# A four-layer graph network in 32 pipelined turns: a small product by rows, new instruction lists, and set-up steps moved into the first turn

## What is computed

```python
# a and d (4 heads of 64)
attn = softmax(where(adj, (q @ k.T) * 64 ** -0.5, -max))
out = (attn @ v) @ Wo + bo
# g (4 heads)
Wh = h @ W[h].T + bW[h]
scores = (Wh @ attn[h]) @ Wh.T
hp = relu(tanh(where(adj, scores, 0)) @ Wh)
ha, hf = concat(hp) @ A_w.T, h @ fc_w.T
coeff = sigmoid(hf @ g1_w.T + ha @ g2_w.T + gbias)
out = hf * coeff + ha * (1 - coeff)
# b (8 heads of 32)
m = x @ map_w.T + map_b
adj_h = (cos(m, m) > 0.1) * softmax(mask(q @ k.T / sqrt(32))) * keep
out = relu(adj_h @ (x @ gcn_map_w.T) @ gcn_W.T / (sum(adj_h) + 1))
```

## Time and profile before

| | us |
|---|---|
| median of 3 runs | 2783.31 |
| the profiled execution | 2784.76 |
| its span, first to last instruction | 2782.9 |
| PE busy in the span | 2662.1 (96%) |
| DVE, ACT, POOL busy | 1972.8, 1398.4, 908.0 |

### The profile page before, as it was taken

How to read it: one execution, slowest core, us unless ns; L and a number is a source line. 1 busy time by engine, 2 the same in 40 slices (tenths; PEclk the granted TensorE clock), 3 DMA queues, 4 the chain that set the end, 5 groups by cost and what they waited for, 6 DMA issues and landing times.

```text
span 2782.9 us, 62595 instructions
## 1 busy us (share of the span) xinstructions
PE 2662.1 (96%) x21777; PEld 2332.1 (84%) x21777; DVE 1972.8 (71%) x6629; ACT 1398.4 (50%) x3861; POOL 908.0 (33%) x979
## 2 busy tenths in 40 slices
PE   8799999999999999999999999999999999999985
PEld 7788888888888888888898888888888889888873
DVE  2367777778777767777777777777877777777764
ACT  1355445555454545544555545554554554554542
POOL 1223233432323333323343233333332434332331
PEclk8899999999999999999999999999999999999996
DMA  4000000000000000000000000000000000000000
GB/s 128 6 3 11 1 11 10 9 9 9 0 9 9 9 9 9 9 0 9 9 9 9 9 0 9 9 9 9 9 4 6 9 9 9 9 9 0 10 5 8
DMA packets 44481, 29.77 MB, mean 11 GB/s; under 512 B 21264, under 2 KB 44048, under 8 KB 44432
## 3 DMA queue, kind: packets, MB, share of 16 engines
q1 hardware_dynamic: 44432, 29.13, 3.6%
HBM read 20.73 MB, written 8.39 MB: 10 GB/s over the span
## 4 chain that ended last, share of the span: by engine, by line
PE 69%; DVE 21%; issue 5%; ACT 3%; DVEq 1%; POOL 0%; DMA 0%; SPq 0%; ACTq 0%; POOLq 0%
PE bank L247 13%; PE bank L249 12%; PE bank L248 12%; PE bank L246 9%; PE bank L1139 4%; PE bank L324 4%; PE bank L236 4%; PE bank L313 3%; PE bank L1121 3%; DVE b L420 2%; DVE x L170 2%; PE bank L1149 2%; DVE arena L420 2%; DVE b L463 2%; DVE l_st L158 2%
## 5 line engine op out<-in xcount | busy, mean ns | idle before, releaser
L1533 POOL TENSOR_TENSOR arena_r<-a,arena_r 128x512 fp32r<-128x512 f32 x128 | 166.0, 1297 | 585.0 <-ACT arena_r L1229 585.0
L1279 ACT ACTIVATE b<-b,s_sh 128x256 f32<-128x256 f32 x512 | 253.7, 499 | 116.0 <-DVE s_sh L420 116.0
L178 POOL TENSOR_SCALAR l_ve<-l_mv 128x2 f32<-128x2 f32 x128 | 29.0, 227 | 864.2 <-DVE l_mv L163 861.8
L247 PE MATMUL bank<-arena_r 128*128 128x256 f32 x1024 | 301.4, 294 | 1.8 <-POOL arena_r L1538 1.8
L248 PE MATMUL bank<-arena_r 128*128 128x256 f32 x1024 | 289.8, 283 | 0.0
L249 PE MATMUL bank<-arena_r 128*128 128x256 f32 x1024 | 289.5, 283 | 0.0
L1538 POOL TENSOR_TENSOR arena_r<-a,arena_r 128x512 fp32r<-128x512 f32 x128 | 165.5, 1293 | 174.6 <-ACT arena_r L1223 172.1
L247 PEld LDWEIGHTS bank<-arena_r 128*128 128x128 f32 x1024 | 195.6, 191 | 22.5 <-issue 20.6
L420 DVE CUSTOM_DVE_ANT_0 b<-bank,s_add 128x256 f32<-128x256 f32 x512 | 183.4, 419 | 39.9 <-PE bank L1121 39.0
L1439 DVE SCALAR_TENSOR_TENSOR b<-bank,b 128x256 f32<-128x256 f32 x512 | 185.1, 416 | 20.3 <-PE bank L1130 20.0
L249 PEld LDWEIGHTS bank<-arena_r 128*128 128x128 f32 x1024 | 196.1, 191 | 0.0
(11 more groups left out here) (273 smaller groups left out, 9099.4 us busy)
## 6 DMA issues: line engine op xcount, KB each, us to landing
x_in<-in_x SPq DMA_DIRECT2D x32, 256.0 KB, 2.8
out<-x SPq DMA_DIRECT2D x32, 256.0 KB, 2.1
adj_a<-in_adj SPq DMA_DIRECT2D x32, 64.0 KB, 2.5
adj_b<-in_adj SPq DMA_DIRECT2D x32, 64.0 KB, 2.4
a<-in_L_gnn_W SPq DMA_DIRECT2D x4, 256.0 KB, 3.3
b<-in_L_gnn_A_w SPq DMA_DIRECT2D x1, 1024.0 KB, 7.1
arena<-in_L_gnn_attn SPq DMA_DIRECT2D x4, 256.0 KB, 7.2
g_b_wh<-in_L_gnn_bW SPq DMA_DIRECT2D x1, 512.0 KB, 9.2
```

The lines of the kernel that those rows point to most:

```text
L247: pe.matmul(out, w[0], x[0], start=first, stop=False)
L1279: last = act.activation(S.e[:, n, it, :], S.e[:, n, it, :], ACT.Exp, bias=S.sh[:, it, h:h + 1], scale=-1.0, accum_out=S.sums[:, it, h:h + 1])
L1533: pool.tensor_tensor(G.wh[h % 2][1], G.whf[:, h % 2, :, :], G.wh[h % 2][0].bitcast(F32), ALU.subtract).then_inc(G.wh_sb.sem, 1)
```

## The change

- `g_c` takes the 8 columns of both halves of `w_c` as the stationary operand and x's halves as the moving one: 4 matmuls give 8 rows of 256. ACT copies the rows, and a new PE stage `g_c_t` has two plain fp32 matmuls that turn them and add the two halves by a selection matrix `C.sel` (8 x 4). DVE's stage is now called `g_c_t`.
- All four lists of `ORDER` are new. On PE the turn begins at `b_transpose_6`; ACT and DVE lists begin elsewhere in the turn than they did, so their lags differ by one.
- `FILL` and `DRAIN` are written-out lists for the turns before and after the hardware loop, which runs t = 4 to 30.
- Of the 34 set-up steps, 21 stay (`EARLY_COPIES`); 13 become stages `w_map` to `w_col_w` of `FILL` and use the four banks of `b` and `d`. PE has them before `a_k` of graph 0, DVE has `w_sem` and `w_col_w` after `a_stats`. What waited for all copies and `wr_loaded` at the end of set-up now waits at `g_x_t` of graph 0 (PE, DVE, ACT) or `a_bias` (POOL). SP loads the `bW` columns with `loads_a`, then the four weights of layer `a`, then `load_a(0)`.

The diff, cut to its core (DVE's and ACT's `late` follow PE's):

```diff
--- before.py
+++ after.py
@@ -49,51 +49,263 @@
 ORDER = {
     "PE": [
-        ("g_ha_3_1", 1), ("g_ha_3_0", 1), ("d_k", 2), ("g_ha_t", 1), ("a_x_t", 0), ("g_gate_x", 1), ("d_q", 2),
-        ("g_gate", 1), ("d_scores_0", 2), ("d_v", 2), ("a_k", 0), ("d_scores_1", 2), ("a_q", 0), ("a_v", 0),
-        ("a_scores_0", 0), ("d_probs_0", 2), ("d_probs_1", 2), ("d_probs_2", 2), ("d_probs_3", 2), ("a_scores_1", 0),
-        ("d_values_0", 2), ("b_x_t", 1), ("a_probs_0", 0), ("a_probs_1", 0), ("d_values_1", 2), ("a_probs_2", 0),
-        ("a_probs_3", 0), ("a_values_0", 0), ("a_values_1", 0), ("d_out", 2), ("a_out", 0), ("b_m", 1), ("b_sem", 1),
-        ("g_adj_t", 0), ("b_q", 1), ("g_x_t", 0), ("b_k", 1), ("g_z_0", 0), ("b_unit_t", 1), ("g_c", 0),
-        ("b_scores_0", 1), ("g_wh_0", 0), ("g_z_1", 0), ("g_s_0", 0), ("b_cos_0", 1), ("g_wh_1", 0), ("g_s_1", 0),
-        ("b_transpose_0", 1), ("b_transpose_1", 1), ("b_transpose_2", 1), ("b_transpose_3", 1), ("g_wh_2", 0),
-        ("b_values_0", 1), ("g_z_2", 0), ("b_scores_1", 1), ("g_p_0", 0), ("g_s_2", 0), ("g_z_3", 0), ("b_cos_1", 1),
-        ("g_p_1", 0), ("b_transpose_4", 1), ("g_wh_3", 0), ("b_transpose_5", 1), ("b_transpose_6", 1), ("g_s_3", 0),
-        ("b_transpose_7", 1), ("g_p_2", 0), ("b_values_1", 1), ("g_hf", 0), ("b_out", 1), ("g_ha_0_1", 0),
-        ("g_ha_0_0", 0), ("g_ha_1_1", 0), ("g_ha_1_0", 0), ("g_p_3", 0), ("g_ha_2_0", 0), ("g_ha_2_1", 0),
-        ("d_x_t", 1),
+        ("b_transpose_6", 2), ("b_transpose_7", 2), ("g_p_3", 1), ("b_values_1", 2), ("g_ha_2_1", 1), ("g_ha_3_1", 1),
+        ("b_out", 2), ("g_ha_2_0", 1), ("g_ha_3_0", 1), ("g_hf", 1), ("g_ha_t", 1), ("g_gate_x", 1), ("a_x_t", 0),
+        ("d_x_t", 2), ("g_gate", 1), ("d_q", 2), ("d_k", 2), ("d_v", 2), ("d_scores_0", 2), ("d_scores_1", 2),
+        ("a_v", 0), ("a_k", 0), ("a_q", 0), ("d_probs_0", 2), ("d_probs_1", 2), ("a_scores_0", 0), ("d_probs_2", 2),
+        ("a_scores_1", 0), ("d_probs_3", 2), ("d_values_0", 2), ("d_values_1", 2), ("a_probs_0", 0), ("a_probs_1", 0),
+        ("b_x_t", 1), ("a_probs_2", 0), ("a_probs_3", 0), ("a_values_0", 0), ("a_values_1", 0), ("d_out", 2),
+        ("a_out", 0), ("b_m", 1), ("b_q", 1), ("b_sem", 1), ("g_x_t", 0), ("g_adj_t", 0), ("b_k", 1), ("g_c", 0),
+        ("g_wh_0", 0), ("g_c_t", 0), ("g_z_0", 0), ("b_unit_t", 1), ("g_wh_1", 0), ("b_scores_0", 1), ("g_z_1", 0),
+        ("g_s_0", 0), ("g_wh_2", 0), ("b_cos_0", 1), ("g_z_2", 0), ("b_transpose_0", 1), ("g_s_1", 0), ("g_p_0", 0),
+        ("b_transpose_1", 1), ("b_transpose_2", 1), ("g_z_3", 0), ("b_transpose_3", 1), ("g_wh_3", 0),
+        ("b_values_0", 1), ("g_s_2", 0), ("b_scores_1", 1), ("g_s_3", 0), ("g_p_1", 0), ("g_ha_0_0", 0),
+        ("g_ha_0_1", 0), ("b_cos_1", 1), ("g_p_2", 0), ("g_ha_1_0", 0), ("b_transpose_4", 1), ("b_transpose_5", 1),
+        ("g_ha_1_1", 0),
     ],
...
     "ACT": [
+        ("a_x_t", 1), ("d_x_t", 3), ("g_gate", 2), ("d_q", 3), ("d_k", 3), ("d_exps_0", 3), ("d_exps_1", 3),
+        ("d_exps_2", 3), ("d_exps_3", 3), ("a_k", 1), ("a_q", 1), ("d_probs_0", 3), ("d_probs_2", 3), ("a_exps_0", 1),
+        ("a_exps_1", 1), ("a_exps_2", 1), ("a_exps_3", 1), ("a_probs_0", 1), ("a_probs_2", 1), ("a_o_copy", 1),
+        ("b_x_t", 2), ("g_x_t", 1), ("b_k", 2), ("g_c", 1), ("b_q", 2), ("g_z_0", 1), ("b_unit_t", 2), ("g_wh_0", 1),
...
     "DVE": [
+        ("g_ha_t", 2), ("g_gate", 2), ("g_mix", 2), ("g_sum", 2), ("a_x_t", 1), ("g_stats", 2), ("d_v", 3),
+        ("d_mask_0", 3), ("d_mask_1", 3), ("d_mask_2", 3), ("g_norm_out", 2), ("d_mask_3", 3), ("d_norm_p_0", 3),
+        ("a_v", 1), ("d_norm_p_1", 3), ("d_probs_1", 3), ("a_mask_0", 1), ("a_mask_1", 1), ("a_mask_2", 1),
+        ("d_probs_3", 3), ("a_mask_3", 1), ("a_norm_p_0", 1), ("a_norm_p_1", 1), ("a_probs_1", 1), ("a_probs_3", 1),
+        ("d_o_copy", 3), ("a_o_copy", 1), ("d_sum", 3), ("b_x_t", 2), ("a_sum", 1), ("a_stats", 1), ("b_m", 2),
+        ("a_norm_out", 1), ("b_square", 2), ("g_x_t", 1), ("b_sem", 2), ("g_adj_t", 1), ("d_stats", 3), ("g_wh_0", 1),
+        ("b_unit", 2), ("g_z_0", 1), ("g_c_t", 1), ("g_wh_1", 1), ("d_norm_out", 3), ("b_mask_0", 2), ("b_mask_1", 2),
...
     "POOL": [
+        ("g_wh_3", 2), ("g_adj", 1), ("b_sums", 3), ("g_a_3", 2), ("b_rstd", 3), ("d_bias", 3), ("g_x_ha", 2),
+        ("b_mask", 2), ("a_bias", 1), ("g_rstd", 2), ("b_keep", 2), ("a_rstd", 1), ("b_inorm", 2), ("d_rstd", 3),
+        ("g_wh_0", 1), ("g_a_0", 1), ("g_wh_1", 1), ("a_mask", 0), ("g_a_1", 1), ("g_wh_2", 1), ("d_mask", 2),
+        ("g_a_2", 1),
     ],
+}
+FILL = {
+    "PE": [
+        ("w_map", 0), ("a_x_t", 0), ("w_qk", 0), ("w_col_r", 0), ("w_col_qk", 0), ("w_sem", 0), ("w_col_w", 0),
+        ("a_k", 0), ("a_q", 0), ("a_v", 0), ("a_scores_0", 0), ("a_scores_1", 0), ("a_probs_0", 0), ("a_probs_1", 0),
+        ("a_probs_2", 0), ("a_probs_3", 0), ("a_values_0", 0), ("a_values_1", 0), ("a_out", 0), ("g_adj_t", 0),
+        ("g_x_t", 0), ("g_c", 0), ("g_z_0", 0), ("g_c_t", 0), ("g_wh_0", 0), ("g_z_1", 0), ("g_wh_1", 0),
+        ("g_s_0", 0), ("g_z_2", 0), ("g_s_1", 0), ("g_wh_2", 0), ("g_p_0", 0), ("g_z_3", 0), ("g_s_2", 0),
...
+DRAIN = {
...
-        G.c_psum, G.c_sb = signal("l1_c_psum"), signal("l1_c_sb")
+        G.c_psum, G.c_sb = signal("l1_c_psum", 2), signal("l1_c_sb", 2)
...
-        G.w_c = split_sb("g_w_c", [P, T, HG])
+        G.w_c_rows = sb("g_w_c", [P, T, 2 * HG], F32R)
+        G.w_c = G.w_c_rows[:, :, 0:HG], G.w_c_rows[:, :, HG:2 * HG]
+        G.c_rows = plain(20)[0:2 * HG, 0, :]
+        C.sel = sb("sel", [2 * HG, HG])
...
+        loads_a += [(W.bw[:, :, h], column(d["L1_gnn_bW"][h])) for h in range(HG)]
...
-        loads_r = whole((W.wq, "L0_gnn_Wq"), (W.wk, "L0_gnn_Wk"), (W.wv, "L0_gnn_Wv"), (W.wo, "L0_gnn_Wo"))
-        columns_s = [(W.bw[:, :, h], column(d["L1_gnn_bW"][h])) for h in range(HG)]
...
+        def w_bank(n):
+            return banks[n % 8] if n < EARLY_COPIES else BB[(n - EARLY_COPIES) % 4]
...
-            pe.wait_ge(ws_loaded, 16 * n_s)
-            for src in (W.map, W.q, W.k):
-                t_done = step(lambda b: pe_transpose_rows(pe, b, src, C.ident))
-            gcn_done = step(lambda b: pe.transpose(b[:, 0:P], W.gcn, C.ident[:, :]))
             step(lambda b: mm_pairs(b, W.fc, lambda kc: W.g1_t[:, kc, :]), needs=g1_done)
             a_done = step(lambda b: columns(b, lambda h, kc, t: W.attn[:, h, kc, t * P:(t + 1) * P],
                                             lambda h, kc: W.bw[:, kc, h:h + 1], HG))
-            step(lambda b: columns(b, lambda h, kc, t: W.r[:, h, kc, t * P:(t + 1) * P], lambda h, kc: W.bw[:, kc, h:h + 1], HG))
-            step(lambda b: mm_pairs(b, W.map, lambda kc: W.q_t[:, kc, :]), needs=t_done)
-            step(lambda b: mm_pairs(b, W.map, lambda kc: W.k_t[:, kc, :]))
-            b_q_done = step(lambda b: columns(b, lambda h, kc, t: W.q_t[:, kc, t * P:(t + 1) * P], lambda h, kc: W.mb[:, kc:kc + 1], 1))
-            step(lambda b: columns(b, lambda h, kc, t: W.k_t[:, kc, t * P:(t + 1) * P], lambda h, kc: W.mb[:, kc:kc + 1], 1))
-            step(sem_weight, needs=gcn_done)
-            step(sem_bias, needs=b_q_done)
-            step(lambda b: columns(b, lambda h, kc, t: W.w[:, h, kc, t * P:(t + 1) * P],
-                                   lambda h, kc: W.ac[:, kc, h:h + 1], HG), needs=b_q_done)
-            step(c_bias)
+            assert a_done == EARLY_COPIES, a_done
+
+            def late(stage):
+                if stage == "w_map":
+                    pe.wait_ge(w_sb, EARLY_COPIES)
+                    pe.wait_ge(ws_loaded, 16 * n_s)
+                    for src in (W.map, W.q, W.k):
+                        step(lambda b: pe_transpose_rows(pe, b, src, C.ident))
+                    step(lambda b: pe.transpose(b[:, 0:P], W.gcn, C.ident[:, :]))
+                elif stage == "w_qk":
+                    step(lambda b: mm_pairs(b, W.map, lambda kc: W.q_t[:, kc, :]), needs=EARLY_COPIES + 3)
+                    step(lambda b: mm_pairs(b, W.map, lambda kc: W.k_t[:, kc, :]))
+                elif stage == "w_col_r":
+                    step(lambda b: columns(b, lambda h, kc, t: W.r[:, h, kc, t * P:(t + 1) * P],
+                                           lambda h, kc: W.bw[:, kc, h:h + 1], HG))
+                elif stage == "w_col_qk":
+                    step(lambda b: columns(b, lambda h, kc, t: W.q_t[:, kc, t * P:(t + 1) * P],
+                                           lambda h, kc: W.mb[:, kc:kc + 1], 1))
+                    step(lambda b: columns(b, lambda h, kc, t: W.k_t[:, kc, t * P:(t + 1) * P],
+                                           lambda h, kc: W.mb[:, kc:kc + 1], 1))
+                elif stage == "w_sem":
+                    step(sem_weight)
+                    step(sem_bias, needs=EARLY_COPIES + 1)
+                elif stage == "w_col_w":
+                    step(lambda b: columns(b, lambda h, kc, t: W.w[:, h, kc, t * P:(t + 1) * P],
```

(84 more changed lines are left out.)

238 lines of the change are left out of this document (178 added, 60 removed), and 127 rows, old and new, of tables (DRAIN, FILL, ORDER).

## The result

The changed kernel took 2699.4 us (median of 4 runs, 2695.7 to 2700.5), the kernel before 2783.5 (2779.0 to 2784.3): ratio 0.9703, interval 0.9687 to 0.9720. The prediction said 2706 in 2668 to 2750. The profiled execution of the changed kernel has a span of 2697.5 us and took 2699.29. First the page: busy time of each engine, then TensorE's granted clock in 40 slices (beside the earlier trace rows).

A forecast was written before the change was run, and what follows sets the result against it. PE's own list bounds steady turns; the ends are chains through all engines. 2784.8 - 72 (thirty turns) + 1 (set-up) - 3 (turn 0) - 3 (turn 1) - 1 (end) = 2706.8, less 1 for the median: 2706, range 2668 to 2750.

The forecast's parts named there:

- Part 1: PE's `g_c` as 4 matmuls plus `g_c_t`: 0.9 against 1.41, a gain of 0.5 a turn (0.2 to 0.6).
- 32 plain ones: Set-up row of one-column plain fp32 matmuls, 4.13 us, 0.13 each; it priced the two matmuls of `g_c_t` at 0.26.
- The rule on weight loads: A load costs by columns, not rows: `g_c_t` pays full loads; pricing by its 8 rows gives 0.2 less a turn.
- Part 2: Stage borders in PE's steady list: regrouping saves 0.8; with the product by rows, the floor goes from 79.4 to 78.2.
- Part 3: Waits of the new steady list, walked: 1.7 a turn; turn 80.0 against 82.4, thirty turns -72.
- rival B: Small gain: DVE's masks and copies interlock with ACT, each late one pushing both; turn 81.2 to 82.2, 2757; chance 0.13.
- Rival C: Slower: DVE's head delays `d_probs_0` and `a_probs_0`; at 4 late the turn is 84, total 2823; chance 0.08.
- 1.5 in hand: DVE's slack at its head, ahead of the masks: 1.5 us, any delay beyond going whole into `d_probs_0` and `a_probs_0`.
- Part 4: Set-up, bound by PE: -2.5 for steps gone, +1.6, +0.4, +1.2 and +0.5 added; sum +1 (-5 to +6).
- Part 5: First turns and end: turn 0 -3 (-8 to +3), turn 1 -3 (-6 to 0), end -1 (-5 to +4).
- steady gains: Turn 1: named with `g_adj_t` as the source of its -3 (-6 to 0).
- Same steps in another order: The end, b(31) then d(31), each a chain: only reordered, -1 (-5 to +4).

The follow-up runs named there:

- experiment 1: Changed kernel with old twelve-matmul `g_c`: 2718.6 us; kernel before with the product by rows alone: 2800.4; kernel before with new steady lists alone: 2719.8.
- experiment 2: Kernel before with the product by rows and `g_wh_0` ahead of `b_scores_0`: 2817.5 us; then DVE's `g_wh_0` and `g_c_t` also moved ahead of masks: 2794.2.
- experiment 3: Changed kernel with `d_scores_0` ahead of `d_v`, and `d_v` and `a_v` between the two score stages: 2747.6 us, ratio 0.9868.
- experiment 5: Changed kernel with DVE's `b_x_t` ahead of `d_sum`: 2691.6 us; on top of it DVE's `d_probs_3` ahead of `a_mask_2`: 2706.0.
- probs_first: Changed kernel with DVE's `b_x_t` ahead of `d_sum`, and also `d_probs_3` ahead of `a_mask_2` on DVE: 2706.0 us, ratio 0.9717.
- gc_cover: Kernel before with the product by rows and `g_wh_0` ahead of `b_scores_0`: 2817.5 us, ratio 1.0119.
- gc_covered: `gc_cover` with DVE's `g_wh_0` ahead of `b_mask_0` and its `g_c_t` ahead of `b_mask_1`: 2794.2 us, ratio 1.0048.
- experiment 6: Changed kernel with `FILL` and `DRAIN` by the old rule: 2714.8 us; kernel with `b_x_t` ahead of `d_sum`, steady list meant for turns 2, 3, 31: 2694.4.

## Why the prediction was right, and where it was not

**The total.** The time, 2699, lies in the range and near the 2706, and the forecast's own condition, a turn of 79.2 to 81.2, is met with 79.72. In part that is luck. Inside the turn, a floor put 0.3 to 0.4 too low and waits put 0.5 to 0.6 too high nearly cancelled. Outside it, the set-up was 1.5 worse and turn 0 0.7 worse than forecast, the 29 turns 3.6, turn 1 1.4 and the end 4.6 better.

**Part 1, the product by rows.** The gain was right, its make-up was not. The pair takes 0.47 + 0.53, and about 0.1 at each of its two borders, 1.2 against the 0.9 of the text. It saves 0.53 a turn in the new lists, forecast 0.5 (experiment 1: 0.35 from the start of `g_c` to `g_z_0`, one of the two waits in it, the rest the other wait, at `b_unit_t`), but 0.4 of that is the two waits that the old product makes there. In the old ones, covered and between other neighbours, it saves 0.61 without a wait (experiment 2).

The term that was mis-sized is the 0.26 for `g_c_t`, which takes 0.53. It was read from "32 plain ones" at 0.13 each, but that step of the set-up writes 16 matmuls (`columns` with 4 heads, line 736 of before), and each stands in the trace as two rows. At 0.26 for one as written, two are 0.52.

What the step lacked: it named only the cover of the new chain to `g_s_0`, and not that the old `g_c` was itself the cover of ACT's copy of `unit_t`. In the old lists that turns a gain of 0.6 into a loss of 0.7. In the new lists `g_wh_1` stands between `b_unit_t` and `b_scores_0`, and nothing is lost. The rule on weight loads holds here: the load for `g_c_t`, 8 partitions deep, took as long as one 128 deep (groups by line, weight loads: busy us, mean ns, idle before).

```profile
L461 PEld LDWEIGHTS bank<-arena_r 128*128 128x128 f32 x1024 | 194.8, 190 | 0.0
...
L1235 PEld LDWEIGHTS bank<-sel,arena 8*128 8x128 f32 x128 | 16.9, 189 | 4.3 <-issue 0.4
L1228 PEld LDWEIGHTS bank<-arena_r,g_w_c 128*8 128x8 f32 x128 | 10.5, 88 | 4.2 <-DVE arena_r L627 2.1
```

That is as the Trainium skill ("TensorE: Matmul & The Clock Gate", LDWEIGHTS) has it, 189 ns for 8 partitions and 190 for 128. In the other direction the trace is less simple: the load of 8 columns took 88 ns, nearly half of that of 128.

**Part 2, the borders.** 0.8 forecast from the lists; the floor fell by 1.0 with the new lists alone (79.8 to 78.8), or by 0.6 where waits of 0.1 are counted (79.4 to 78.8), so 0.8 lies between. The absolute floor was put at 78.2 and is 78.5 to 78.6. The borders of experiment 3 cost 0.33, forecast 0.2 to 0.3. But the step hid something: the lists were read as moving like to like, and experiment 3 shows that putting `d_scores_0` back ahead of `d_v` costs 1.44 more in waits, because `d_v` covers ACT's copy of k.

**Part 3, the waits.** The sum was 1.7 and is 1.1 to 1.2. Right in place and near in size: `a_probs_0` (0.4, is 0.31), `d_x_t`/`g_gate` (0.3, is 0.22), `b_transpose_4` gone. Too small: `d_values_1` (0.1, is 0.25) and `b_m` (0.1, is 0.36), where the walk overlooked that DVE stands idle ahead of `d_sum` with `b_x_t` queued behind it (experiment 5). Not there: `a_probs_2` and `a_values`, priced 0.5. "Each late one pushes both" (rival B) is what `probs_first` shows, but for an order that the change doesn't have.

**Rival C.** The "1.5 in hand" of DVE was wrong: 0.27 ahead of `d_v` and 0.43 ahead of `a_mask_0`. The walk counted only the masks, though the same text listed `d_scores_1` waiting for `d_v`. Had DVE come to `d_v` 2 us later than its rows say, 1.7 of the 2.7 us that a turn gained would have gone (an estimate from the 0.27). C did not happen because the rows of DVE hold, not because of slack.

**Part 4, the set-up.** +1 was forecast, +2.5 is the difference of the two profiles. Other kernels show a wide spread. The same set-up code reached `a_k` of graph 0 between 66.7 and 70.6 in the profiles of eight kernels with the new set-up in full, and at 64.3, 64.3, 64.4, 64.6 and 58.4 in five with the old set-up. So the new one is longer, by 2.2 at the least and 6 in the means. Up to `a_x_t` of graph 1, so with turn 0, it is 132.7 against 132.5 in the two profiles compared, and 133.5 against 128.4 in the means of the eight and of the four with the old lists, which spread from 123.5 to 132.5. Set-up and turn 0 together, forecast 2 shorter, are not shorter; whether they are 0 or 5 us longer stays open. The windows for the set-up from 30 us on: the changed kernel and the kernel with `b_x_t` ahead of `d_sum`, which have the new set-up; then `gc_cover` and `gc_covered` (the first and second kernel of experiment 2), which have the old one.

```profile
30.00:66.73 36.73, 33.37 (x185) 31.63 (x183) 8.86 (x20) 5.23 (x10) 7.33 (x6) 0.70 0.11 30
```
```profile
30.00:70.56 40.56, 37.55 (x191) 35.65 (x189) 9.14 (x20) 5.82 (x11) 7.33 (x6) 0.66 0.11 30
```
```profile
30.00:64.57 34.57, 32.26 (x186) 30.04 (x185) 10.21 (x24) 5.34 (x10) 11.24 (x12) 0.72 0.12 26
30.00:58.38 28.38, 26.07 (x179) 24.38 (x177) 9.52 (x23) 5.11 (x10) 11.22 (x12) 0.86 0.09 26
```

The granted clock (third number from the end), a mean of stretches at 1.2 and at 2.4 GHz, goes with the difference: 0.70 and 0.66 with the new set-up, 0.72 and 0.86 with the old. The same 32 rows of column matmuls take 4.07 us in the first kernel and 6.83 in the second, in TensorE's timelines:

```profile
61.18 4.07 PE L960 MATMUL bank<-n_ac,a 128*128 128x1 f32 x32
```
```profile
62.26 6.83 PE L983 MATMUL bank<-n_ac,a 128*128 128x1 f32 x32
```

One step is right by its row: the product that waits for the copy of `g1`, +1.6 in the text, waits 1.90 at 33.99 where it waited 0.48. Whether a reordered step makes the clock lower was not tried. Executions of one kernel differ by as much (2779.0 to 2784.3 before, 2695.7 to 2700.5 after), and the profile of `gc_covered` is of its fastest execution, 2789.3 with a median of 2794.2. So part of the spread may lie between executions and not between kernels; with one profile of each this is not shown.

**Part 5, the ends.** Turn 0's -2.3 (forecast -3) can't be told from the spread: from `a_k` on, the other three kernels with old lists took 64.2, 64.5 and 65.1 against 68.2 for the kernel before and 66.0 for the changed one. Turn 1 was right in size (-4.4 for -3, in its bounds), but not by "steady gains": with the new steady lists by the old rule it takes 77.3 (without the product by rows) and 78.7 (experiment 6), beside 77.7 before and 73.3 with its own sequence.

The last stretch is the worst term by size: -8.0 for -3.4. Of the 4.6 us beyond, 1.1 lie in the last steady turn and 3.5 behind `g_gate_x` (101.1 to 96.6, forecast -1). "Same steps in another order" was the step that was mis-sized. What takes its place is known in part. From `g_gate_x` of graph 31 on, the kernel with the new steady lists alone (experiment 1) and the one of experiment 6 run the very same lists by the old rule, yet the windows show 97.27 us for the first and 100.11 for the second:

```profile
2620.91:2718.18 97.27, 61.38 (x383) 46.19 (x380) 49.28 (x179) 29.07 (x88) 16.32 (x22) 0.81 0.02 6
2613.24:2713.35 100.11, 64.12 (x383) 47.73 (x381) 49.22 (x179) 29.05 (x88) 16.34 (x22) 0.74 0.02 6
```

What differs in these rows is the granted clock, 0.81 and 0.74. Four kernels with the old lists end in 101.1 to 102.0 at 0.75, eight with the own sequence for the last stages in 96.4 to 98.4 at 0.77 to 0.80. So the new steady order by itself brings 1.0 to 3.8 us, and the own sequence between 0.7 and 3.5 more; how much of either comes by way of the clock was not tried.

## What to carry to other kernels

In a list that is bound by one engine, every stage is also the cover of some other engine's step. Before a stage is shortened or moved, ask what ends during it, not only what it waits for: the same product was worth -0.53 a turn in one list and +0.68 in another. And slack from a walk is to be read at each consumer: the smallest counts, here 0.27 at `d_v`, where the walk had looked only at the masks and found 1.5. A row's count is also to be held against the code before a price is taken from it: 32 rows were 16 matmuls.

## What was not expected of the hardware

`g_c_t` is written as two plain fp32 matmuls and stands in the trace as four (x128 for 32 graphs), 8*128 with 4 columns streamed, 0.53 from its first start to the next stage, so 0.13 each, with 0.21 from the last start ahead of it. The forecast had taken 0.13 for each of two. The trace of before had the same all along: a score stage writes 4 plain fp32 matmuls and shows x8, the column step of the set-up writes 16 and shows x32; the transposes, 4 written, show x4. And the set-up reached `a_k` at 64.6 in one kernel and at 58.4 in another with the same set-up code, at a granted clock of 0.72 and 0.86.
